# Seven maxima of the second unit moved from in front of the first scores into the first unit's cycles (softmax attentions)

## The reference, cut to what matters

```python
q = split_heads(layernorm(x) @ wq.T + bq)      # 4 x 16 x 512 x 16
k = split_heads(ctx @ wk.T + bk)               # 4 x 16 x 1601 x 16
v = split_heads(ctx @ wv.T + bv)
attn = softmax(einsum('bhqd,bhkd->bhqk', q, k) / sqrt(16), axis=-1)
x = x + merge_heads(einsum('bhqk,bhkd->bhqd', attn, v)) @ wo.T + bo
```

## Time and profile before

| | |
|---|---|
| median of 3 runs | 2636.61 us (2634.14 to 2639.84) |
| the profiled execution | 2633.87 us |
| its span | 2632.1 us |
| mean granted TensorE clock | 0.975 |
| busy: PE, DVE, ACT, POOL | 95%, 62%, 59%, 14% |

### The profile page before, as it was taken

The page is one execution under the profiler, slowest core; times in us unless marked ns, Lnnn a source line. Parts: engine busy times, 40 slices in busy tenths (PEclk is TensorE's granted clock), DMA queues, the critical chain, the costliest instruction groups (busy, mean ns, idle before and its releaser), DMA issues.

```text
span 2632.1 us, 46589 instructions
## 1 busy us (share of the span) xinstructions
PE 2511.5 (95%) x18460; PEld 1252.8 (48%) x18464; DVE 1626.1 (62%) x2991; ACT 1544.5 (59%) x2621; POOL 362.0 (14%) x351
## 2 busy tenths in 40 slices
PE   6999999999899889999999999999999999999987
PEld 3434344343377768886333333278633443434433
DVE  6878788879387774442112221067687888888854
ACT  1777777777701221111797978932147777777773
POOL 3020200200012401221001010021402002020001
PEclk8999999999999999999999999999979999999998
DMA  5423334232210001001753535110133433234200
GB/s 125 76 32 45 58 44 76 28 49 27 64 43 17 1 25 48 1 1 54 113 74 65 89 53 72 49 53 1 24 52 63 54 61 51 41 49 54 36 1 33
DMA packets 68636, 125.13 MB, mean 48 GB/s; under 512 B 20979, under 2 KB 45630, under 8 KB 64966
## 3 DMA queue, kind: packets, MB, share of 16 engines
q1 hardware_dynamic: 67270, 119.73, 27.4%
q10 hardware_dynamic: 1152, 2.44, 0.4%
HBM read 41.59 MB, written 2.10 MB: 17 GB/s over the span
## 4 chain that ended last, share of the span: by engine, by line
PE 82%; DVE 9%; ACT 4%; issue 2%; POOL 1%; ACTq 1%; SPq 0%; DMA 0%; POOLq 0%; DVEq 0%
PE psum L203 39%; PE psum L764 21%; PE psum L214 13%; PE psum L2152 6%; DVE mpart L956 4%; ACT probs L831 3%; PE psum L309 1%; DVE x L1440 1%; PE psum L774 0%; PE psum L2145 0%; ACTq L1084 0%; ACTq L1091 0%; PE psum L783 0%; POOL kp_lo L1032 0%; DVE mparts L969 0%
## 5 line engine op out<-in xcount | busy, mean ns | idle before, releaser
L831 ACT ACTIVATE probs<-psum 128x512 f32<-128x512 f32 (+3 forms) x2080 | 1268.1, 686 | 279.0 <-PE psum L203 270.7
L956 DVE TENSOR_REDUCE mpart<-psum 128x2 f32<-128x804 f32 x1024 | 970.9, 990 | 220.3 <-PE psum L203 206.9
L764 PE MATMUL psum<-probs,vt 128*17 128x512 f32 (+1 forms) x4992 | 650.6, 600 | 3.9 <-ACT probs L831 3.1
L203 PE MATMUL psum<-qst,kst 64*128 64x512 f32 (+3 forms) x2496 | 602.5, 439 | 18.1 <-ACT probs L831 7.7
L203 PE MATMUL psum<-kst,qst 62*128 62x402 f32 x2048 | 466.3, 411 | 27.6 <-DVE mpart L956 26.6
L203 PEld LDWEIGHTS psum<-qst,kst 64*128 64x128 f32 (+3 forms) x2496 | 282.9, 182 | 378.2 <-issue 202.8
L203 PEld LDWEIGHTS psum<-kst,qst 62*128 62x128 f32 x2048 | 226.1, 191 | 306.7 <-DVE mpart L956 192.6
L764 PEld LDWEIGHTS psum<-probs,vt 128*17 128x17 f32 (+1 forms) x4992 | 92.1, 96 | 212.8 <-issue 176.6
L214 PE MATMUL psum<-wv,ctxT 128*32 128x256 f32 (+1 forms) x2448 | 171.5, 399 | 4.8 <-DVE kp_lo L937 2.6
L214 PE MATMUL psum<-ctxT,wk 128*32 128x512 f32 (+1 forms) x1536 | 146.7, 508 | 9.7 <-DMA ctxT<-in_ctxT 8.8
L2200 ACT ACTIVATE inner<-psum 128x512 f32<-128x512 f32 x32 | 19.2, 599 | 199.2 <-PE psum L2152 199.2
(11 more groups left out here) (339 smaller groups left out, 2607.7 us busy)
## 6 DMA issues: line engine op xcount, KB each, us to landing
kst<-kp_hi SPq DMA_DIRECT2D x144, 200.1 KB, 6.9
ctxT<-in_ctxT SPq DMA_DIRECT2D x36, 512.0 KB, 5.4
kst<-kp_lo SPq DMA_DIRECT2D x72, 200.1 KB, 6.5
qst<-qp_hi SPq DMA_DIRECT2D x144, 64.0 KB, 2.5
kst<-kp_hi SPq DMA_DIRECT2D x84, 100.1 KB, 3.4
qst<-qp_lo SPq DMA_DIRECT2D x72, 64.0 KB, 2.4
kst<-kp_lo SPq DMA_DIRECT2D x42, 100.1 KB, 3.4
stage<-in_L_ffn_W SPq DMA_DIRECT2D x16, 256.0 KB, 4.0
```

The source lines that it names most:

```text
L203: last = e.matmul(dst, lhsT, rhs, start=i == 0, stop=i == len(pairs) - 1)
L764: t = e.matmul(c.bank(self.acc)[32 * h:32 * h + VW, :], self.vt[0:kn, kc, self.head(g, h), :], p[0:kn, h % self.wide, :], start=kc == 0, s ...
L831: e.activation(self.probs[n % slots][0:kn, :, :], c.psum[0:kn, k:k + self.wide, :], ACT.Exp if softmax else ACT.Sigmoid, scale=DH ** -0.5) ...
L956: e.tensor_reduce(self.mpart[:, :, p * (SEQ // P) + qt, i], c.psum[:, k:k + 2, 0:MAX_WIDTH], AX.X, ALU.max).then_inc(c.drained(k), 1)
```

## The change

A table `FIRST_UNIT` gives the first unit of each softmax attention (u = 0) cycles of its own. They hold 6, 6, 6, 6, 6, 5 and 4 maxima, 39 in all: the 32 of unit 1, and then the seven of unit 2 that the first unit held before. The seven maxima of unit 1 in front of the first scores are gone. `max_close` of unit 1 now comes right behind its last maximum, in cycle 5, and `max_turn` of unit 1 in the middle of cycle 6. Nothing is computed more or less often.

```diff
+FIRST_UNIT = ("sssmsmsmsmsmsmf",
+              "msmssvmssmsvssmmf",
+              "msmssvmssmsvssmmff",
+              "msmssvmssmsvssmmff",
+              "smsmsvmsssvmssmffm",
+              "ssvmssmvssmfmssfm",
+              "svmsmsmsmv")
...
-        steps = [step for letter in ORDERS[self.softmax][u % GROUPS][i] for step in [next(taken[letter], None)] if step]
+        order = FIRST_UNIT[i] if self.softmax and u == 0 else ORDERS[self.softmax][u % GROUPS][i]
+        steps = [step for letter in order for step in [next(taken[letter], None)] if step]
...
         if self.softmax and u + 1 < UNITS:
-            if i == 4:
+            if u == 0:
+                if i == 5:
+                    steps.insert(steps.index(self.max_steps(1)[-1]) + 1, ("max_close", f, 1))
+                elif i == 6:
+                    steps.insert(len(steps) // 2, ("max_turn", f, 1))
+            elif i == 4:
                 steps.append(("max_close", f, u + 1))
             elif i == 5:
                 steps.insert(len(steps) // 2, ("max_turn", f, u + 1))
...
+        if u == 0:
+            first = sum(order.count("m") for order in FIRST_UNIT[:i])
+            return (self.max_steps(1) + self.max_steps(2)[:7])[first:first + FIRST_UNIT[i].count("m")]
         ahead, first = (u + 1, 7 + 5 * i) if i < 5 else (u + 2, 5 * (i - 5))
...
             put(self.max_steps(0) + [("max_close", f, 0)], -1.2, -0.2, first_maxima)
-            put(self.max_steps(1)[:2], -0.2, -0.15, maxima)
             put([("max_turn", f, 0)], -0.14, -0.14, misc)
-            put(self.max_steps(1)[2:7], -0.13, 0, maxima)
```

## The result

| | before | changed |
|---|---|---|
| median | 2636.68 us (2634.14 to 2645.93, 6 runs) | 2659.15 us (2651.12 to 2662.31, 6 runs) |
| the profiled execution | 2633.87 us | 2658.19 us |
| its span | 2632.1 us | 2656.4 us |
| mean granted clock in it | 0.975 | 0.970 |

The ratio is 1.0075, with a 95% interval of 1.0061 to 1.0089: slower, as forecast, but by some 20 us where +10 was forecast, and above the range's 2653.

What follows compares the result with a forecast made beforehand. PE was taken to bound unit 0, with DVE close behind. Terms -2.0 + 6.4 + 7.7 - 1.3 = +10.8 us on 2633.87 gave 2644.7, stated as a median of 2646 us; range 2637 to 2653.

Steps and rivals of the forecast that it cites:

- A: Start of unit 0's first scores: PE waits for the rows alone, scores 0.95 and 1.05 us earlier, gain 2.0 us.
- B: First scores to unit 0's last values step: moved maxima cost PE and DVE waits, +3.25 and +3.1, together +6.4 us.
- C: Last values step to unit 1's first scores: late turn, new PE wait for rows, +4.2 and +3.5, together +7.7 us.
- D: Unit boundary: PE's waits for DVE's queue go, 0.65 us each, -1.3 us.
- The clock falls in the new wait: Rival at unit 1's first scores: 4.4 us lost once or twice, 2650 to 2655; chance 0.07.
- busy at over 90%: Sign that the forecast is right: DVE's busy share in unit 0 after the change.
- 1.5 to 3: Sign that the forecast is right: us PE waits for rows at unit 1's first scores, in both attentions.
- lower bound of B: First scores to unit 0's last values step: at least +1.2 us, PE's price alone.
- Rival 1: Unit 0: DVE's idle time takes the seven reductions; +3.4 to +5, 2639 to 2642; chance 0.22.
- Rival 2: Unit 1's first scores: rows wait for the whole context load; +10.0 there, 2648; chance 0.18.
- Rival 3: After unit 0's first scores the clock rises earlier: -8.8 us for both attentions, 2631; chance 0.08.

Runs made afterwards that it cites:

- e_front_only: Kernel before with the seven maxima in front taken away and done nowhere, old cycles and turn; 2636.97 us against 2637.27.
- e_late_all: Kernel before with the turn in the middle of cycle 6 instead of cycle 5 in every unit; 2776.51 us, ratio 1.0520.
- e_early_close: Changed kernel with 7, 7, 6, 6, 6, 4 and 3 maxima in its cycles, close and turn as before the change; 2649.09 us.
- e_sooner_rows: Changed kernel with unit 1's turn at the start of cycle 6 and the context load issued behind unit 1's rows; ratio 1.0050.
- e_fill_wait: Changed kernel with seven extra 512-column matmuls, results unread, in PE's wait ahead of unit 1's first scores; 2658.52 us, ratio 1.0079.
- c_after: The changed kernel run again with no edit, as base for the others on their chip; 2656.72 us against 2637.27.
- e_late_turn: Kernel before, close and maxima where they were, only unit 1's turn moved to the middle of cycle 6; 2653.16 us.
- e_rows_first: Changed kernel with the context load issued behind unit 1's rows, at the end of cycle 6; 2657.64 us.
- e_start6_rows: Kernel before with unit 1's turn at the start of cycle 6 and the context load issued behind unit 1's rows; ratio 1.0041.
- e_turn_sooner: Changed kernel with unit 1's turn at the start of cycle 6, right behind the context load; 2656.32 us, ratio 1.0068.
- e_warm_front: Kernel before with four 110-column matmuls added at every maximum in front of the first scores; 2702.98 us, ratio 1.0257.

## Why the prediction was right and wrong

**A, the start of the scores: right.** Forecast -0.95 and -1.05 us, measured -0.77 and -0.80 to the scores' weights; to the matmul itself it is 1.1, as in e_front_only, which shows it alone.

**B, to the last values step: right in sum.** Forecast +3.25 and +3.1, measured 39.62 - 37.13 = +2.5 and 37.97 - 34.99 = +3.0. In f = 6 the chain shows where, here the second of three boundaries:

```profile
1968.03 0.98 PE psum L778 x8
...
1971.69 1.91 DVE mpart L970 x2
1973.65 0.69 PE psum L210 x4
1974.34 0.98 PE psum L778 x8
```

From pv step to pv step a cycle takes 6.31 us where it took 5.65, and DVE's two reductions stand in the chain between, as forecast (also at 1965.40 and 1978.00). That is 0.20 for the maximum and 0.45 of waiting, forecast 0.6. Up to the first pv step cycle 0 costs 1.1 us more, forecast 0.7.

**C, the late turn and its wait: right in sum.** Forecast +4.2 and +3.5, measured (47.94 - 39.62) - 4.28 = +4.0 and (45.80 - 37.97) - 4.30 = +3.5, with waits of 1.38 and 1.34 us at the low end of 1.4 to 2.2. The delay by the context load, taken at 0.7 each, was 0.06 (4.41 us against 4.35 in front). Instead the turn came 0.2 and 0.4 us later than summed, and from turn to scores 4.8 us passed in place of 4.45: here two misses cancel, and that is luck.

**D, given back at the boundary: wrong, and small.** Forecast -1.3. In f = 6, where no fall disturbs it, the lag behind the kernel before, counted from the turn, is 5.7 us at unit 1's first scores and 5.8 at `accs`: nothing came back. PE is busy 9.31 of 10 us there, where it had 9.35.

```profile
2000.00:2010.00 10.00, 9.31 (x65) 3.61 (x64) 9.19 (x11) 8.64 (x18) 0.00 (x0) 1.00 0.98 120
```

**The step that failed is in the rivals.** "The clock falls in the new wait" had no term in the sum and a chance of 0.07, on the ground that "the wait is some 2 us only, and PE was at 1.00 through the gaps of the boundary". The gaps of the boundary are many small ones, 0.66 us in 10 us; the wait is one piece. That this is what tells them apart is argued. e_late_all speaks for it, and e_early_close too: from 114 to 120 PE is idle there for 1.1 of 6 us, in pieces of 0.43 at most, at a clock of 1.00. Against it stand the falls of e_sooner_rows (f = 0) and e_fill_wait (f = 6), which had no idle piece over 0.7 us ahead; what sets off a fall stays open. The fall came in 1 of 2 places in the first profile, in 2 of 2 in c_after and e_late_turn. Its size had been right (4.4 us forecast for one, 3.4 to 4.2 measured). The forecast's terms A, B and C, as measured, add up to +11.5 us; with c_after's two falls (4.2 and 3.5) that is about 19, of a measured 20.1. The losses of the two halves of the change don't simply add up: late turn +16.1 and cycles +11.3 would be 27, the change has 20. PE's wait is shorter in the change (1.4 us against 2.4 to 2.6), with a maximum more behind the turn. Of the distance between the two single profiles (24.3 us), some also lies in stages that nobody touched: the profiled execution of before was a lucky one, 2.7 us under its median, and the changed one took 7 us longer from `accs` of f = 0 to the turn of f = 6.

Of the signs named ahead, DVE "busy at over 90%" in unit 0 failed: it was 87% and 83% (41.54 of 47.94, 37.98 of 45.80), and the forecast's own numbers, 35.04 + 6.7 in 47.5, give 88%. The waits of 1.38 and 1.34 us also lie just under the named 1.5 to 3. The lower bound of B is a little off by its own terms: PE's price alone is 1.0 - 0.2 and 1.0 - 0.2 - 0.65, together 0.95 and not 1.2.

**Rival 1**, DVE's idle time takes the maxima: fell; five kernels with 39 maxima in the cycles all have a rest of 6 to 11 us, and at unit 1's first scores, before any fall, they are 5.0 to 6.5 us late in each attention. What the norm adds to B in f = 0 was not tried by itself. **Rival 2**, rows behind the load: not decisive in the changed kernel, a true mechanism half a cycle sooner. **Rival 3**, an earlier rise of the clock: in f = 0 the clock went back to 1.00 at about 77, 9 us after the first scores (8.8 before), so it fell. The length varies from one execution to the next; see e_front_only. The window from 76 to 78 has 0.75 and the next one 1.00:

```profile
76.00:78.00 2.00, 2.00 (x19) 1.19 (x15) 1.25 (x2) 1.21 (x3) 0.00 (x0) 0.75 0.95 102
78.00:80.00 2.00, 2.00 (x23) 0.80 (x15) 1.97 (x5) 1.56 (x4) 0.00 (x0) 1.00 1.12 160
```

No version here beats the kernel before; e_front_only, which leaves seven maxima out, only equals it.

## What to carry to other kernels

Moving work off an idle gap that a transfer covers anyway gains only what lies behind the landing (here 1.6 us), and pays the full price where the work goes. When a change makes the bound engine wait in one piece, ask what its clock does behind the wait: here a wait of 1.4 us cost less than the fall behind it (3.5 to 4.2). And for a small transfer that someone will wait for, look at what was issued shortly ahead of it on the same queue, and from when.

## What the runs showed of the hardware

- Of 23 idle pieces of PE of 1.8 to 3.6 us at the first scores of a unit, 21 had a fall to 1.2 GHz for 3.4 to 17.1 us; of 5 of 1.34 to 1.38 us, 3 (e_rows_first, c_after and the changed kernel, all in f = 0); of 9 of 0.88 to 1.02 us, 2 (e_start6_rows, e_turn_sooner). Of 15 first scores of unit 1 with no such piece, 2 had one (e_fill_wait, e_sooner_rows). A fall of 10.2 us cost 3.4 to 4.2 us.
- Records of a busy PE didn't raise the clock: 42 us of them at 1.2 GHz in e_warm_front, nearly all matmuls of maxima and the small ones put beside them. The Trainium skill ("TensorE: Matmul & The Clock Gate", What's actually happening) has activity release the throttle; in these 42 us the trace doesn't show that.
- Four DMAs of 4 KB let the scores start 4.4 us after the copy ahead of them, but 6.1 and 7.1 us after it when a load of 1.6 MB had been issued 1.6 us ahead of the copy on the same queue. With the load issued 3.3 us ahead it was 4.4 us once and 4.8 once.
- Stages that were not touched differed by up to 7 us between single profiled executions, by low stretches of 3.4 us that come and go.
